# A decoder layer whose routed expert results are added to their token rows by accumulating transfers, with half of the shared expert moved ahead of the routed tiles

## The chip, the cores and the metric

The kernel runs on one NeuronCore of a Trainium2 chip. The metric is the device time of one execution in microseconds (us), taken as the median of several runs. One further execution was recorded by the hardware profiler, and every duration below is from that one. The engines are named as in the profile: PE is the matmul engine (PEld its weight loads), DVE the vector engine, ACT the scalar engine, POOL the GpSimd engine, SP the engine that only issues transfers. An engine's name with a q behind it (SPq, ACTq) is its queue of transfers.

## What is computed

One decoder layer on 32 blocks of 128 tokens, 256 wide: causal attention with 16 heads, a retention-like second attention, and a mixture of experts, each added to its input and normalised. The change concerns only the last part:

```python
x = _layernorm(x + _L0_attn_ref(x, L0_attn_qkv_weights), axis=-1)
x = _layernorm(x + _L0_xattn_ref(x, ctx_1024, ctx_1024, ...), axis=-1)
x = _layernorm(x + _L0_ffn_ref(x, ...), axis=-1)
...
# _L0_ffn_ref: one shared expert, and the best 2 of 8 routed experts for each token
hs = jnp.einsum('bsd,ndf->nbsf', x, sw1) + sb1[:, None, None, :]
shared_out = jnp.einsum('nbsf,nfd->bsd', _swiglu(hs), sw2) + sb2.sum(0)
probs = jax.nn.softmax(x @ gate_w + gate_b, axis=-1)
topk_probs, topk_idx = jax.lax.top_k(probs, TOP_K)
cw = jnp.sum(jax.nn.one_hot(topk_idx, N_EXPERTS, dtype=x.dtype) * topk_probs[..., None], axis=2)
hr = jnp.einsum('bsd,edf->ebsf', x, rw1) + rb1[:, None, None, :]
out_e = jnp.einsum('ebsf,efd->ebsd', _swiglu(hr), rw2) + rb2[:, None, None, :]
routed_out = jnp.einsum('ebsd,bse->bsd', out_e, cw)
return shared_out + routed_out
```

All data are float32.

## The kernel before, in words

Every engine has its own program, written out by hand in the order in which it runs; semaphores join them. There are four stages.

**Attention**, about 0 to 401 us. Blocks of 128 tokens go through a pipeline of steps n = -2 to 40; step n works on several blocks at once, each at another depth. At the end of the pipeline a block has its second layernorm result x2, which goes as a packet (256 values, the row number of its first result, its two expert numbers) to two rows of the DRAM tensor `sent`, one for each of its experts, by indirect transfers of POOL (L640). The row with x2 and the bias sb2 goes to `x2_dram`, the transposed one to `x2T_dram`.

**The gap**, about 401 to 463 us. The last steps n = 33 to 40 empty the pipeline: they route the last blocks, and in steps 33 to 36 PE puts one piece (`shared_half`, L795) of the shared expert's first group between them. A group q is 4 blocks, 512 tokens; there are 8. Then DVE counts the rows of each expert (15 dependent operations, `planned`, L1447 to L1464), and PE computes the first layer of group 1.

**Routed tiles**, about 463 to 692 us. `sent` is worked through in 71 tiles of 128 rows, each of one expert. For tile i: a load of ACT's queue brings the packets (`xg`), PE transposes them (L976), ACT copies them out (L1184), PE multiplies by rw1 (`hidden`, L990), DVE adds the bias (L1486), ACT takes the Silu (L1179), POOL multiplies (`product`, L671), PE transposes (L983), ACT copies (L1189), PE multiplies by rw2 (`result`, L1001), DVE adds the bias (`yg`, L1505), and POOL writes the 128 result rows to their places in the DRAM tensor `back` by an indirect transfer (`send_back`, L674). The tiles overlap: in PE's queue turn_x(i+1), turn_h(i-1), result(i-2) and hidden(i+1) follow each other. Two `back` transfers may be under way at once.

**The tail**, 692 us to the end. For each group, the results (`got`, 1 MB) and the rows x2 are loaded, DVE multiplies and sums them with the token's weights (`weighted`, L1548), adds the shared expert's output (`add_shared`, L1566), takes the moments, POOL the root (L697), ACT normalises and SP stores. PE computes the shared expert's first layer of groups 2 to 7 (`shared`, L795) and second layer of groups 0 to 7 (`output`, L1039) here, with the two engines handing each other PSUM banks.

## Time and profile before

| | us |
|---|---|
| median of 3 runs | 769.59 (768.74 to 775.72) |
| the profiled execution, its own time | 775.48 |
| its span from first to last instruction | 773.6 |
| PE busy | 705.6 (91%) |
| DVE busy | 499.1 (65%) |
| ACT busy | 410.3 (53%) |
| POOL busy | 319.1 (41%) |

The profiled execution took 5.9 us more than the median of the runs. A sum made against it is carried to the median by taking off that difference. Matmuls are pipelined, so a busy PE is not PE at its peak.

### The profile page before, as it was taken

Reading aid. Unit: us, or ns where it says so; the run is one execution under the profiler, and the core shown is the slowest. Engines: PE = TensorE matmul, PEld = TensorE weight load, DVE = VectorE, ACT = ScalarE, POOL = GpSimd, SP = SyncE. Lnnn points to the kernel's source line nnn. Section 1 sums busy time; section 2 is a strip of 40 time slices with the busy share of each in tenths; the row PEclk is TensorE's granted clock in tenths of the full one; section 3 lists DMA queues with packets and bytes.
Section 4 is the critical chain, followed back from the end, with each engine's and each line's share of the span. In section 5 each row is a group of like instructions: output and inputs, shape, how many; then the busy total and the mean of one; then the engine's idle time right before and its main releaser. Section 6 shows DMA issues by size and latency. Waiting matters only on the chain.

```text
span 773.6 us, 19404 instructions
## 1 busy us (share of the span) xinstructions
PE 705.6 (91%) x5464; PEld 533.1 (69%) x5465; DVE 499.1 (65%) x1568; ACT 410.3 (53%) x1167; POOL 319.1 (41%) x451
## 2 busy tenths in 40 slices
PE   6978899999999999999987639999999999999993
PEld 6857788888888888888875315666666666665453
DVE  3555678888988888898866432444444444438985
ACT  0268688888888888888851102333333333312233
POOL 1001233335554554455455542555555555541111
PEclk9999999999999999999999677999999999999998
DMA  8644462213332332333271432422222222229962
GB/s 290 253 145 157 138 223 74 83 57 106 102 97 82 103 109 77 100 101 108 85 228 62 151 124 88 152 83 88 83 87 89 82 89 84 86 61 320 302 215 81
DMA packets 77032, 97.54 MB, mean 126 GB/s; under 512 B 12320, under 2 KB 63264, under 8 KB 75936
## 3 DMA queue, kind: packets, MB, share of 16 engines
q1 hardware_dynamic: 59920, 68.21, 28.0%
q0 software_dynamic: 6816, 19.00, 6.8%
q10 hardware_dynamic: 10224, 9.42, 4.4%
q8 instruction: 39, 0.64, 0.3%
q14 instruction: 33, 0.27, 0.1%
HBM read 60.02 MB, written 36.56 MB: 125 GB/s over the span
## 4 chain that ended last, share of the span: by engine, by line
PE 67%; issue 14%; DVE 5%; SPq 5%; DMA 4%; POOL 2%; ACT 1%; POOLq 0%; ACTq 0%; DVEq 0%
PE ps L990 16%; PE ps L1001 8%; PE ps L777 5%; PE ps L765 4%; PE ps L855 4%; PE ps L742 4%; PE ps L787 4%; PE ps L879 3%; PE ps L745 3%; PE ps L858 3%; PE ps L976 2%; PE ps L983 2%; DMA attn_only<-in_ctx 2%; DVE products L1263 2%; PE ps L865 2%
## 5 line engine op out<-in xcount | busy, mean ns | idle before, releaser
L1079 ACT ACTIVATE prob<-ps,nmax 128x128 f32<-128x128 f32 x512 | 146.8, 378 | 30.2 <-DVE nmax L1253 30.2
L990 PE MATMUL ps<-first_use,xgT 128*128 x284 | 137.3, 607 | 1.3 <-ACT xgT L1184 1.2
L1486 DVE TENSOR_TENSOR hid<-ps,attn_only 128x512 f32<-128x512 f32 x71 | 49.1, 692 | 93.8 <-PE ps L990 93.8
L1184 ACT COPY xgT<-ps 128x256 f32<-128x256 f32 x71 | 26.5, 373 | 133.9 <-PE ps L976 131.7
L1253 DVE TENSOR_REDUCE nmax<-ps 128x4 f32<-128x512 f32 x128 | 82.2, 685 | 22.7 <-PE ps L765 21.0
L671 POOL TENSOR_TENSOR gate_h<-hid,sil 128x256 f32<-128x256 f32 x71 | 50.9, 717 | 100.3 <-DVE result_row L1499 82.7
L1086 ACT COPY pT<-ps 128x512 f32<-128x512 f32 x128 | 76.7, 599 | 19.2 <-PE ps L777 14.5
L621 POOL TENSOR_TENSOR rot<-products 128x128 f32<-128x128 f32 x128 | 61.2, 499 | 60.9 <-DVE products L1263 57.8
L777 PE MATMUL ps<-tf,prob 128*128 128x128 f32 x512 | 78.6, 276 | 5.8 <-ACT pT L1086 5.7
L990 PEld LDWEIGHTS ps<-first_use,xgT 128*128 128x128 f32 x284 | 54.7, 194 | 41.1 <-issue 37.5
L640 POOL DMA_INDIRECT sent<-packets,pos x64 | 63.6, 994 | 37.1 <-PE ps L765 22.8
L674 POOL DMA_INDIRECT back<-yg,result_row x71 | 71.8, 1011 | 13.8 <-issue 12.3
L1001 PE MATMUL ps<-first_use,ghT 128*128 x284 | 74.0, 383 | 0.5 <-ACT ghT L1189 0.5
L777 PEld LDWEIGHTS ps<-tf,prob 128*128 128x128 f32 x512 | 59.3, 141 | 11.7 <-issue 5.4
L795 PE MATMUL ps<-prob,sw_sb 128*128 128x512 f32 x128 | 62.5, 639 | 3.9 <-DMA prob<-x2T_dram 2.7
L976 PEld LDWEIGHTS ps<-tf,xg 128*128 128x128 f32 x142 | 19.1, 144 | 54.9 <-issue 54.2
L1505 DVE TENSOR_TENSOR yg<-ps,attn_only 128x256 f32<-128x256 f32 x71 | 30.2, 425 | 39.3 <-PE ps L1001 36.7
L1001 PEld LDWEIGHTS ps<-first_use,ghT 128*128 128x128 f32 x284 | 48.3, 190 | 4.9 <-issue 0.9
L1263 DVE TENSOR_TENSOR products<-ps,tf 128x256 f32<-128x256 f32 x128 | 46.3, 404 | 6.0 <-PE ps L879 2.0
L795 PEld LDWEIGHTS ps<-prob,sw_sb 128*128 128x128 f32 x128 | 25.5, 203 | 33.4 <-issue 29.2
L653 POOL TENSOR_TENSOR rstd<-mv,neg_half 128x1 f32<-128x1 f32 x32 | 17.7, 552 | 67.5 <-DVE mv L1271 67.5
L1359 DVE CAST ps<-tb 128x512 f32<-128x512 bf16 x62 | 42.0, 682 | 2.1 <-ACT prob L1079 2.1
(135 smaller groups left out, 1390.2 us busy)
## 6 DMA issues: line engine op xcount, KB each, us to landing
xg<-sent ACTq DMA_DIRECT2D x68, 129.5 KB
first_use<-back SPq DMA_DIRECT2D x8, 1024.0 KB, 8.2
k_dram<-first_use SPq DMA_DIRECT2D x4, 1024.0 KB, 4.3
attn_only<-in_x_turned SPq DMA_DIRECT2D x32, 128.0 KB, 2.7
attn_only<-k_dram SPq DMA_DIRECT2D x256, 16.0 KB
attn_only<-in_x SPq DMA_DIRECT2D x32, 128.0 KB, 2.6
attn_only<-in_ctx SPq DMA_DIRECT2D x32, 128.0 KB, 2.6
first_use<-in_L_ffn_rw SPq DMA_DIRECT2D x8, 512.0 KB, 5.0
```

The lines of the kernel that those rows point to most:

```text
L621: eng.tensor_tensor(rot[:, t % 2, m + e, :], ra[:, t % 2, m + e, :], rb[:, t % 2, m + 1 - e, :], ALU.add).then_inc(done, 1)
L640: eng.indirect_dma_start(sent, bass.IndirectOffsetOnAxis(ap=pos[:, t, j:j + 1], axis=0), packets[:, t % SLOTS, :], None).then_inc(sent_in[ ...
L671: eng.tensor_tensor(gate_h[:, r, :], hid[:, r, FFN:2 * FFN], sil[:, r, :], ALU.mult).then_inc(gh_set, 1)
L674: eng.indirect_dma_start(back, bass.IndirectOffsetOnAxis(ap=result_row[:, slot:slot + 1], axis=0), yg[:, slot % 2, :], None).then_inc(yg_o ...
L777: mm = eng.transpose(PROBT[:, n * P:(n + 1) * P], prob[:, t % 2, 4 * u + n, :], ident)
L795: mm = eng.matmul(ps[:, bank0 + 2 * f + half, :].rearrange("p (b t) -> p b t", b=QB), sw1_sb[:, c, cols:cols + P], x2T4[:, r, :, c, :], st ...
L990: mm = eng.matmul(ps[:, r, :], xgT[:, r, c, :], rw1_sb[:, bass.ds(e * (DC * 2 * FFN) + c * 2 * FFN, 2 * FFN)], start=(c == 0), stop=(c == ...
L1001: mm = eng.matmul(ps[:, 4 + r, 0:D], ghT[:, r, c, :], rw2_sb[:, bass.ds(e * (FFN // P * D) + c * D, D)], start=(c == 0), stop=(c == FFN // ...
L1079: ins = eng.activation(prob[:, t % 2, 4 * u + n, :], SCORE[u][:, n * P:(n + 1) * P], ACT.Exp, bias=nmax[:, t % 2, 4 * u + n:4 * u + n + 1])
L1086: eng.copy(pT[:, u, :, :].rearrange("p n t -> p (n t)"), PROBT).then_inc(pT_set, 1)
L1253: eng.tensor_reduce(nmax[:, t % 2, 4 * u:4 * u + 4], SCORE[u].rearrange("p (h j) -> p h j", j=P), AX_X, ALU.max, negate=True).then_inc(max ...
L1263: eng.tensor_tensor(into[:, t % 2, m:m + 2, :], source, table[:, m:m + 2, :], ALU.mult).then_inc(done, 1)
```

## The change

**Results.** The tensor `back` goes. A new DRAM tensor `total` has one row for each token (and 128 rows for padding); it holds x2 plus sb2 first, and for groups 0 to 3 (`EARLY` is 4) the shared expert's output too. DVE and POOL work out each row's weight from two more values in the packet, ACT multiplies the tile's result by it (`weighted`, into `yw`), and POOL's indirect transfer adds the 128 rows to `total` (`add_rows`, with an accumulate operation). Since two tiles can hold the same token, a tile's transfer is issued only when the one before has landed: `wait_rows(i)` waits for `row_added` to reach 16*i. The issue comes three tiles behind `product`, one tile later than before.

**Shared expert.** PE computes both layers of groups 0 to 3 before the tiles: between the last steps of the pipeline (`shared_between`, steps 33 to 39) and beside DVE's counting. DVE adds them to the rows `kept` in SBUF, and SP stores these. Groups 4 to 7 come behind the tiles.

**Tail.** When all 71 additions have landed SP loads `total` in 8 pieces of 512 KB. Nothing is left to be weighted; DVE adds the shared output of groups 4 to 7 alone, and takes the moments of all 8.

```diff
-PACKET = D + 3
+PACKET = D + 5
...
+        total = nc.dram_tensor("total", (ROWS + P, D), F32).ap()
...
-        back = nc.dram_tensor("back", (PADDING + TILES * P, D), F32).ap()
...
+            def store_kept(q):
+                eng.wait_ge(sy_added, 2 * q + 2)
+                eng.dma_start(total[q * QB * S:(q + 1) * QB * S, :].rearrange("(b p) d -> p b d", p=P),
+                              kept[:, q * QB:(q + 1) * QB, :]).then_inc(kept_stored, 16)
+            for q in range(EARLY - 2):
+                store_kept(q)
             eng.wait_ge(plan_step, PLAN_STEPS)
...
+            eng.wait_ge(row_added, 16 * TILES)
+            for q in range(NQ):
+                eng.dma_start(fin[:, q * QB:(q + 1) * QB, :],
+                              total[q * QB * S:(q + 1) * QB * S, :].rearrange("(b p) d -> p b d", p=P)).then_inc(fin_in[q], 16)
...
-            def product(i, r, more=True):
+            def product(i, r):
                 eng.wait_ge(sil_set, i + 1)
                 after(eng, gh_turned, i - 1)
-                if more:
-                    eng.wait_ge(yg_set, i - 1)
-                    eng.wait_ge(packet_row, i - 1)
                 eng.tensor_tensor(gate_h[:, r, :], hid[:, r, FFN:2 * FFN], sil[:, r, :], ALU.mult).then_inc(gh_set, 1)
-            def send_back(slot):
-                eng.indirect_dma_start(back, bass.IndirectOffsetOnAxis(ap=result_row[:, slot:slot + 1], axis=0),
-                                       yg[:, slot % 2, :], None).then_inc(yg_out[slot % 2], 16)
-            for i in range(2):
-                product(i, i, more=False)
-            for i in range(2, 4):
+            def tile_weight(i, slot):
+                eng.wait_ge(part_set, i + 1)
+                eng.tensor_tensor(weight[:, slot:slot + 1], weight_part[:, slot:slot + 1], xg[:, slot, D + 3:D + 4],
+                                  ALU.add).then_inc(weight_set, 1)
+            def wait_rows(i):
+                eng.wait_ge(yw_set, i + 1)
+                eng.wait_ge(packet_row, i + 1)
+                after(eng, row_added, 16 * i)
+            def add_rows(slot):
+                eng.indirect_dma_start(total, bass.IndirectOffsetOnAxis(ap=result_row[:, slot:slot + 1], axis=0),
+                                       yw[:, slot % 2, :], None, compute_op=ALU.add).then_inc(row_added, 16)
+            for i in range(3):
                 product(i, i % 2)
-                send_back(i - 2)
+                tile_weight(i, i)
+            for r in range(2):
+                eng.wait_ge(x2_stored[r], 16 * (B - EARLY * QB) // 2)
+            eng.wait_ge(idle_sent, 32)
+            eng.wait_ge(kept_stored, 16 * EARLY)
+            product(3, 1)
+            wait_rows(0)
+            tile_weight(3, 3)
+            add_rows(0)
             with eng.Fori(1, TILES // 4) as k:
                 for n in range(4):
                     product(4 * k + n, n % 2)
-                    send_back((n - 2) % 4)
+                    wait_rows(4 * k + n - 3)
+                    tile_weight(4 * k + n, n)
+                    add_rows((n + 1) % 4)
             for i in range(TILES // 4 * 4, TILES):
                 product(i, i % 2)
-                send_back((i - 2) % 4)
-            for i in range(TILES - 2, TILES):
-                eng.wait_ge(yg_set, i + 1)
-                eng.wait_ge(packet_row, i + 1)
-                send_back(i % 4)
-            def root(q, r):
+                wait_rows(i - 3)
+                tile_weight(i, i % 4)
+                add_rows((i - 3) % 4)
+            for i in range(TILES - 3, TILES):
+                wait_rows(i)
+                add_rows(i % 4)
...
+            def shared_hidden(q, f, bank):
+                if q > 0:
+                    eng.wait_ge(sgh_set, 2 * (q - 1) + f + 1)
+                for half in range(2):
+                    shared_half(q, f, half, bank)
+            def shared_output(q, bank):
+                eng.wait_ge(sgh_set, 2 * q + 2)
+                for i in range(2):
+                    if 0 < q < EARLY:
+                        eng.wait_ge(sy_added, 2 * (q - 1) + i + 1)
+                    for b in (2 * i, 2 * i + 1):
+                        for c in range(FFN // P):
+                            mm = eng.matmul(ps[:, bank + i, b % 2 * D:(b % 2 + 1) * D], sgh[:, q % 2, c, b * P:(b + 1) * P],
+                                            sw2_sb[:, c, :], start=(c == 0), stop=(c == FFN // P - 1))
+                    mm.then_inc(sy_made, 1)
+            def shared_between(n):
                 if n == B + 1:
-                    eng.wait_ge(x2T4_in[0], 16)
                     eng.wait_ge(ffn_in, 16 * (2 + 2 * NE))
                     eng.wait_ge(expd, 4 * B)
-                    shared_half(0, 0, 0)
+                    shared_hidden(0, 0, 0)
                 if n == B + 2:
-                    shared_half(0, 0, 1)
+                    shared_hidden(0, 1, 2)
                 if n == B + 3:
-                    shared_half(0, 1, 0)
+                    shared_hidden(1, 0, 0)
                 if n == B + 4:
-                    shared_half(0, 1, 1)
+                    eng.wait_ge(pT_set, 4 * B)
+                    eng.wait_ge(att_set, B)
+                    shared_output(0, 4)
+                if n == B + 5:
+                    shared_hidden(1, 1, 2)
+                if n == B + 6:
+                    shared_hidden(2, 0, 0)
+                if n == B + 7:
+                    shared_output(1, 4)
...
+            shared_hidden(2, 1, 2)
+            shared_hidden(3, 0, 0)
+            shared_output(2, 4)
+            shared_hidden(3, 1, 2)
+            shared_output(3, 4)
             eng.wait_ge(base_set, len(GROUPS) + 1)
-            shared(1, 0, 1, 4)
-            eng.wait_ge(sgh_set, FFN // P)
+            eng.wait_ge(res2_set, B)
+            eng.wait_ge(sgh_set, 2 * EARLY)
+            eng.wait_ge(sy_added, 2 * EARLY)
...
             result(TILES - 2, TILES % 2, two_before)
-            output(0, 0, 2)
+            eng.wait_ge(sgh_set, 2 * EARLY)
+            shared_half(EARLY, 0, 0, 6)
             turn_h(TILES - 1, (TILES - 1) % 2)
-            output(0, 0, 3)
             result(TILES - 1, (TILES - 1) % 2, before)
-            eng.wait_ge(yg_set, TILES - 1)
-            output(0, 0, 1)
+            shared_half(EARLY, 0, 1, 6)
+            eng.wait_ge(hid_set, TILES)
+            shared_hidden(EARLY, 1, 0)
+            shared_hidden(EARLY + 1, 0, 6)
+            eng.wait_ge(xgT_set, TILES)
+            eng.wait_ge(ghT_set, TILES)
+            shared_output(EARLY, 2)
+            shared_hidden(EARLY + 1, 1, 0)
+            shared_hidden(EARLY + 2, 0, 6)
             eng.wait_ge(yg_set, TILES)
-            output(0, 0, 0)
-            for r in range(2):
-                shared(2 + r, 1, r)
-                outputs(1 + r, 1 - r)
-            with eng.Fori(2, NQ // 2) as k:
-                for r in range(2):
-                    shared(2 * k + r, k, r)
-                    outputs(2 * k + r - 1, 1 - r)
-            outputs(NQ - 1, 1)
+            shared_output(EARLY + 1, 4)
+            shared_hidden(EARLY + 2, 1, 0)
+            shared_hidden(EARLY + 3, 0, 6)
+            eng.wait_ge(sy_added, 2 * EARLY + 2)
+            shared_output(EARLY + 2, 2)
+            shared_hidden(EARLY + 3, 1, 0)
+            eng.wait_ge(sy_added, 2 * EARLY + 4)
+            shared_output(EARLY + 3, 4)
...
+            def weighted(i, r, slot):
+                eng.wait_ge(yg_set, i + 1)
+                eng.wait_ge(weight_set, i + 1)
+                after(eng, row_added, 16 * (i - 1))
+                eng.activation(yw[:, r, :], yg[:, r, :], ACT.Copy, scale=weight[:, slot:slot + 1]).then_inc(yw_set, 1)
...
+            def add_shared(q, bank):
+                if q < EARLY:
+                    eng.wait_ge(x2b_set, (q + 1) * QB)
+                else:
+                    eng.wait_ge(fin_in[q], 16)
+                for i in range(2):
+                    rows = (kept if q < EARLY else fin)[:, q * QB + 2 * i:q * QB + 2 * i + 2, :].rearrange("p b d -> p (b d)")
+                    eng.wait_ge(sy_made, 2 * q + i + 1)
...
-            def pad_rows(i, slot, loads):
+            def weight_parts(i, slot, loads):
                 eng.wait_ge(xg_in[slot], loads * 16)
-                eng.scalar_tensor_tensor(out=pad_shift[:, slot:slot + 1], in0=xg[:, slot, D:D + 1], scalar=float(PADDING),
-                                         in1=tile_rows[:, bass.ds(i, 1)], op0=ALU.is_ge, op1=ALU.mult).then_inc(pad_shifted, 1)
-                eng.scalar_tensor_tensor(out=packet_at[:, slot:slot + 1], in0=tile_e[:, bass.ds(i, 1)],
-                                         scalar=xg[:, slot, D + 2:PACKET], in1=xg[:, slot, D:D + 1],
-                                         op0=ALU.is_equal, op1=ALU.add).then_inc(pad_shifted, 1)
-            def packet_rows(i, slot):
-                eng.wait_ge(pad_shifted, 2 * i + 2)
-                eng.tensor_tensor(result_row[:, slot:slot + 1], pad_shift[:, slot:slot + 1], packet_at[:, slot:slot + 1],
-                                  ALU.add).then_inc(packet_row, 1)
-            def out_y(i, r, sent_before, e):
+                eng.scalar_tensor_tensor(out=weight_part[:, slot:slot + 1], in0=tile_e[:, bass.ds(i, 1)],
+                                         scalar=xg[:, slot, D + 2:D + 3], in1=xg[:, slot, D + 4:D + 5],
+                                         op0=ALU.is_equal, op1=ALU.mult).then_inc(part_set, 1)
+            def rows_of(i, slot):
+                after(eng, row_added, 16 * (i - 3))
+                eng.tensor_copy(result_row[:, slot:slot + 1], xg[:, slot, D:D + 1]).then_inc(packet_row, 1)
+            def out_y(i, r, e):
                 eng.wait_ge(yg_made, i + 1)
-                after(eng, yg_out[r], sent_before * 16)
+                after(eng, yw_set, i - 1)
...
+            def moments(q):
+                if q < EARLY:
+                    eng.wait_ge(fin_in[q], 16)
+                for b in range(QB):
+                    if q >= EARLY:
+                        eng.wait_ge(sy_added, 2 * q + b // 2 + 1)
+                    eng.bn_stats(bn3[:, q, b, :], fin[:, q * QB + b, :]).then_inc(bn3_set, 1)
+                eng.wait_ge(bn3_set, (q + 1) * QB)
+                for b in range(QB):
+                    eng.bn_aggr(mv3[:, q, b, :], bn3[:, q, b, :]).then_inc(mv3_set, 1)
+                eng.wait_ge(mv3_set, (q + 1) * QB + q)
+                eng.tensor_scalar(var3[:, q, :], mv3[:, q, :, 1], EPS, None, ALU.add).then_inc(mv3_set, 1)
...
+            shared_gate(4, 0, 6)
+            shared_gate(4, 1, 0)
+            shared_gate(5, 0, 6)
+            moments(0)
+            shared_gate(5, 1, 0)
+            moments(1)
+            shifts(0)
+            add_shared(4, 2)
```

The order on **POOL, in the loop over the tiles**, two tiles of the four in a turn before and one now. `gate_h` is the product, `back` and `total` the transfers; in the new kernel `tile_parts` holds `gate_h`, `oT` holds `yw`. Before:

```order
L671 TENSOR_TENSOR gate_h<-hid,sil 128x256 [waits packet_row,yg_set,gh_turned]
L674 DMA back<-yg,result_row 17280x256
L665 REGISTER_ALU
L671 TENSOR_TENSOR gate_h<-hid,sil 128x256 [waits yg_set,packet_row,gh_turned,sil_set]
L674 DMA back<-yg,result_row 17280x256
```

Now:

```order
L636 REGISTER_ALU
L638 TENSOR_TENSOR tile_parts<-tile_parts 128x256 [waits gh_turned,sil_set]
L411 REGISTER_ALU [waits packet_row,yw_set]
L642 TENSOR_TENSOR weight<-weight_part,xg 128x1 [waits part_set,row_added]
L654 DMA total<-oT,result_row 4224x256
```

The wait for the transfer before (`row_added`) and a small addition now stand between the product and the transfer.

The order on **PE, in steps 35 to 39, around the last two routing counts** (L938 before, L944 now). Before:

```order
L925 MATMUL ps<-gate_w_sb,x2T 128x8
L938 MATMUL ps<-picks,tb 128x16 [waits gc_set,base_set,picks_set]
L942 MATMUL ps<-picks,tb 128x8
L946 MATMUL ps<-picks,tb 128x8 x2
L938 MATMUL ps<-picks,tb 128x16 [waits gc_set,base_set,picks_set]
L942 MATMUL ps<-picks,tb 128x8
L946 MATMUL ps<-picks,tb 128x8 x2
L795 MATMUL ps<-prob,sw_sb 128x512 [waits x2T4_in1,base_set]
```

Now (L784 is the first layer, L804 the second):

```order
L931 MATMUL ps<-gate_w_sb,x2T 128x8
L784 MATMUL ps<-prob,sw_sb 128x512 [waits sgh_set]
L784 MATMUL ps<-prob,sw_sb 128x512 x3
L944 MATMUL ps<-picks,tb 128x16 [waits gc_set,base_set,picks_set]
L948 MATMUL ps<-picks,tb 128x8
L952 MATMUL ps<-picks,tb 128x8 x2
L784 MATMUL ps<-prob,sw_sb 128x512 [waits x2T4_in2,sgh_set]
L784 MATMUL ps<-prob,sw_sb 128x512 x3
L804 MATMUL ps<-sw_sb,tile_parts 128x256 [waits sy_added,sgh_set]
L804 MATMUL ps<-sw_sb,tile_parts 128x256 x3
L804 MATMUL ps<-sw_sb,tile_parts 128x256 [waits sy_added]
L804 MATMUL ps<-sw_sb,tile_parts 128x256 x3
```

Behind the gate's matmul of the last block two first-layer pieces and a second layer now stand ahead of the last count.

The order on **DVE, in the counting** (`planned`): before, its 15 operations stood in a row and the gates (L1472) behind them. Now a gate (L1389) stands inside:

```order
L1509 CAST counts<-counts_i 128x8 [waits plan_step]
L1389 SCALAR_TENSOR_TENSOR tile_parts<-ps,sb_sb,pT 128x512 [waits sy_made,ssil_set,plan_step]
L1511 TENSOR_TENSOR upto<-counts,tf 128x64
L1513 TENSOR_REDUCE counts<-upto 128x8 [waits plan_step]
L1514 TENSOR_SCALAR counts<-counts 128x8 [waits plan_step]
L1515 TENSOR_TENSOR passed<-counts,tf 128x568 [waits plan_step]
L1517 TENSOR_REDUCE tile_f<-passed 128x71 [waits plan_step]
L1389 SCALAR_TENSOR_TENSOR tile_parts<-ps,sb_sb,pT 128x512 [waits sy_made,ssil_set,plan_step]
L1519 TENSOR_SCALAR tile_e<-tile_f 128x71
L1520 CAST tile_expert<-tile_e 1x71 [waits plan_step]
```

Two gates now stand between the counting operations, each of which waits for ACT and so for PE.

## Rows read from the trace of the kernel before

**Rows 1.** The page's busy line and its row of PE's granted clock (40 slices).

```profile
PE 705.6 (91%) x5464; PEld 533.1 (69%) x5465; DVE 499.1 (65%) x1568; ACT 410.3 (53%) x1167; POOL 319.1 (41%) x451
...
PEclk9999999999999999999999677999999999999998
```

**Rows 2.** Busy time by stretch: PE, PEld, DVE, ACT, POOL, clock, DMA share, GB/s.

```profile
401.00:463.00 62.00, 36.30 (x170) 22.25 (x170) 28.62 (x124) 8.05 (x17) 32.77 (x42) 0.81 0.37 121
463.00:503.00 40.00, 38.39 (x127) 21.80 (x128) 14.56 (x53) 11.58 (x33) 15.28 (x18) 0.87 0.40 119
503.00:684.00 181.00, 181.00 (x709) 111.84 (x708) 81.38 (x295) 61.91 (x177) 101.97 (x118) 1.00 0.28 85
684.00:692.30 8.30, 7.76 (x35) 5.59 (x34) 2.38 (x9) 1.05 (x3) 4.98 (x6) 1.00 0.14 49
692.30:762.00 69.70, 66.51 (x210) 39.24 (x208) 58.99 (x182) 20.01 (x36) 7.48 (x8) 1.00 0.72 243
762.00:773.60 11.60, 0.00 (x0) 0.00 (x0) 2.53 (x12) 4.15 (x8) 1.03 (x2) 0.72 0.26 90
```

**Rows 3.** Timeline of one tile: start, us, engine, line.

```profile
522.34 1.01 POOL L674 DMA_INDIRECT back<-yg,result_row  x1 [0.16 <-issue]
...
523.48 1.88 PE L990 MATMUL ps<-first_use,xgT 128*128 x4
...
523.81 0.42 DVE L1505 TENSOR_TENSOR yg<-ps,attn_only 128x256 f32<-128x256 f32 x1 [0.42 <-PE ps L1001]
...
524.48 0.72 POOL L671 TENSOR_TENSOR gate_h<-hid,sil 128x256 f32<-128x256 f32 x1 [1.12 <-DVE result_row L1499]
...
525.36 1.01 POOL L674 DMA_INDIRECT back<-yg,result_row  x1 [0.16 <-issue]
...
526.50 1.88 PE L990 MATMUL ps<-first_use,xgT 128*128 x4
```

**Rows 4.** Timeline: the last `back` transfer, and SP's first instruction that waited for it.

```profile
691.74 0.96 POOL L674 DMA_INDIRECT back<-yg,result_row  x1 [1.53 <-DVE yg L1505]
...
694.16 0.91 SPq L540 DMA_DIRECT2D first_use<-back  x2
```

**Rows 5.** POOL's groups by shape: busy us, mean ns of one, idle before.

```profile
L621 POOL TENSOR_TENSOR rot<-products 128x128 f32<-128x128 f32 x128 | 61.2, 499 | 60.9 <-DVE products L1263 57.8 <-issue 2.7
L671 POOL TENSOR_TENSOR gate_h<-hid,sil 128x256 f32<-128x256 f32 x71 | 50.9, 717 | 100.3 <-DVE result_row L1499 82.7 <-ACT sil L1179 17.5
...
L653 POOL TENSOR_TENSOR rstd<-mv,neg_half 128x1 f32<-128x1 f32 x32 | 17.7, 552 | 67.5 <-DVE mv L1271 67.5
```

**Rows 6.** Timeline: the first loads of `xg` from DRAM, and PE, which waited for the first.

```profile
460.87 2.60 SPq L554 DMA_DIRECT2D xg<-sent  x3
...
463.04 0.66 PE L976 MATMUL ps<-tf,xg 128*128 128x128 f32 x2 [11.81 <-DMA xg<-sent]
```

**Rows 7.** Timeline of the gap.

```profile
433.19 3.32 PE L795 MATMUL ps<-prob,sw_sb 128*128 128x512 f32 x4
...
437.74 1.28 ACT L1156 ACT_TABLE_LOAD   x1
...
440.88 0.19 PE L938 MATMUL ps<-picks,tb 128*128 128x16 bf16 x1 [2.06 <-issue]
...
454.40 0.22 DVE L1464 TENSOR_TENSOR tile_row<-tile_f,tf 1x71 int32<-1x71 f32 x1 [0.67 <-DVE tile_f L1463]
...
458.66 0.69 ACT L1156 ACTIVATE pT<-ps,sb_sb 128x512 f32<-128x512 f32 x1 [10.15 <-remote]
```

**Rows 8.** Timeline of the tail on PE: first layer, second layer, and the last one.

```profile
737.73 7.03 PE L795 MATMUL ps<-prob,sw_sb 128*128 128x512 f32 x16
...
744.60 3.62 PE L1039 MATMUL ps<-sw_sb,products 128*128 128x256 f32 x16
...
754.92 7.07 PE L1039 MATMUL ps<-sw_sb,products 128*128 128x256 f32 x32
```

**Rows 9.** DVE's groups from 440 us on: the weighting of half of the results.

```profile
L1548 DVE SCALAR_TENSOR_TENSOR first_use<-first_use,cw 128x256 f32<-128x256 f32 x32 | 13.3, 479 | 2.0 <-DMA first_use<-back 2.0
```

426 lines of the change are left out of this document (182 added, 244 removed).

## The prediction

> **What bounds the kernel now.** Read the busy line first: PE is busy for 705.6 of 773.6 us, and its granted clock is full but for three of the forty slices, around 430 to 480 us [rows 1]. Then go by stages [rows 2]. In the attention and in the tiles PE does not rest: from 503 to 684 us it is busy for all of the 181 us, at clock 1.00. A tile takes 12 matmul passes (four of L990, four of L1001, two each of L976 and L983), so 709 passes are 59.1 tiles, and a tile takes 181 / 59.1 = 3.06 us. The start of one tile's L990 to the next tells the same, 526.50 - 523.48 = 3.02 [rows 3]. POOL is busy for 102 of these 181 us; nobody waits for its transfers. Two places are not at PE's limit. In the gap, 401 to 463 us, PE is busy for 36.3 of 62 us at a mean clock of 0.81. In the tail it is busy for 66.5 of 69.7 us, but DVE is busy for 59.0 of them, and 11.6 us follow in which PE has ended and the last group is normalised and stored [rows 2]. So the tail costs 762.0 + 11.6 - 692.3, 81.3 us, and PE's share of it is what the change moves.
>
> **The tail gets shorter: -27 us.** Now PE computes first layers of six groups and second layers of eight there. The first layer of a group takes 7.03 us and the second 3.62 [rows 8]. Afterwards four groups are left: 4 x (7.03 + 3.62) = 42.6 us. They start in the slots at 687.5 that now hold group 0's second layer. Added to them are the last two tiles' results and transposes with the wait for ACT's copy, about 2.4 us, and one wait for the last Silu and gate, about 1.8. PE then ends at 687.5 + 46.8 = 734.3 where it ends at 762.0 now: 27.7 us less, and I take 27. The 11.6 us behind it stay: moments, root, normalising and storing of one group are the same. DVE loses the weighting, 64 operations of 479 ns, 30.7 us (half of them are in [rows 9]), so it cannot bound the tail. What is new there is the load of `total`, 4.2 MB in eight pieces, behind the last addition. Its cover is PE's queue: groups 4 and 5 need no row of it for their first layers, some 20 us. If the cover fails, because the last additions land late, DVE stands at `moments(0)` with the gates of group 5 queued behind it, and PE waits for these; I price that at 0 to 12 us and take 0.
>
> **The gap gets longer: +9 us.** Ahead of the last routing count PE now has two more first-layer pieces, 3.5 us each by half of 7.03, and one second layer, 3.6: 10.6 us [rows 8]. Their cover is PE's idle time there, 2.06 us ahead of that count [rows 7] and about as much ahead of the one before; 6.5 us remain, and DVE's counting waits for them. The Silu pieces now alternate with the Exp of the routing. A change of table costs 1.28 us [rows 7]; there is one now and there will be five. Of the four new ones I put 2 us on the path. Two gates stand inside the counting, 0.75 us each, and the first waits for PE's piece and ACT: 3 us. Against it, the first-layer passes at 433.19 took 3.32 us for four [rows 7], where four passes of the same width take 1.88 in a tile [rows 3]: PE had been idle and was at the lower clock level (1.2 GHz). With more work it may stay at 2.4 GHz, and I give 3 us back. The sum is 6.5 + 2 + 3 - 3 = 8.5, taken as 9. Behind the counting stand DVE's gate, a second layer and an addition, some 6.5 us; the way from its last operation at 454.40 to the first tile at 463.04 [rows 7, 6] takes 8.6 us anyway and hides them. The bounds are +3 and +16: ACT's Silu at 458.66 stood for 10.15 us on something the profile calls remote [rows 7], and if that hits a gate inside the counting, 7 us come on top.
>
> **The tiles: +43 us.** PE's work for a tile is unchanged. ACT has one more operation of 0.4 us, DVE one fewer; neither is near its limit (62 and 81 of 181 us, rows 2). The two new values in a packet and the small operations that fill them in the attention cost nothing that can be seen: PE bounds it. What is new is a ring. An addition may be issued only when the one before has landed, and in POOL's queue the next product stands behind that wait. One turn of the ring is: the transfer from its issue to its landing, POOL's small addition L642, and 0.16 us ahead of the issue [rows 3]. The last `back` transfer was issued at 691.74, and SP went on at 694.16: 2.42 us [rows 4]. A POOL operation takes 717 ns on 256 columns and 499 on 128 [rows 5], which leaves 0.28 for one column; a root of one column takes 0.55. So the ring would turn in 2.42 + 0.16 + 0.28 to 0.55 = 2.86 to 3.13 us if an adding transfer were as quick as a writing one. I take 3.0. That is PE's 3.06 already, with nothing to spare.
>
> An adding transfer must also read its 128 rows. The trace has none. From below this costs nothing, if the read lies beside the other parts of the transfer. It can't be a gain, since the same bytes are written. From above it is a whole trip to DRAM: 128 packets were loaded in 463.04 - 460.87 = 2.17 us [rows 6]. I take a third, 0.7 us: issue, first fetch and the receipt are shared with the write, and only the rows' own way is added. The ring then turns in 3.7 us, and the stage grows by (3.7 - 3.06) x 68 = 43.5 us (three of the 71 additions start before the ring is full). The product of the next tile, 0.72 us [rows 3], fits into the transfer's flight, so it adds nothing. DVE's `rows_of` and ACT's `weighted` wait for the same landings; from a landing through bias, Silu and product to the next issue there are two turns, so they do not set the pace.
>
> The start of the tiles, 463 to 503 us, ran at 0.87 of the clock and lost some 7 us with its filling [rows 2]. A PE that comes busy out of the gap loses less: -2 us.
>
> The Trainium skill says of a transfer on POOL's path that it costs about 2.0 us plus its bytes at 436 GB/s (DMA: Bandwidth & Descriptors, "Anatomy of one DMA"); for 128 KB an estimate by that page is 2.3 us, and [rows 4] show 2.42 with the waiting engine's own delay. The same page ("SDMA does more than copy") says that the units which add are inline with the data stream. By that rule the addition would be free but for the read, and the time that of the first rival below. Its rules for kernel authors say too that an accumulate reads its destination and writes it later, so that the next must wait for the earlier one's semaphore; no row here shows such a transfer.
>
> **The sum.** 43.5 - 27 + 9 - 2 = +23.5. The profiled execution took 775.5 us, so 799.0; it was 5.9 above the median, which makes 793.
>
> **Rivals.** *The additions hide* (chance 0.27): the read lies beside the write, the ring turns in at most PE's 3.06 us, and 9 - 27 - 2 = -20 remain: 750 us. For it speaks that the ring without the read is 2.86 at the least; against it that this leaves 0.2 us. *The ring is only just too slow* (0.13): 3.2 to 3.4 us a turn, +10 to +23 - 20, that is 760 to 773. At 3.35 us gain and loss are equal. *The additions are serial* (0.18): each row is read, added and written before the next, or POOL needs longer to write the descriptors. With the whole trip of 2.17 on top of 3.0 the ring turns in 5.2 us: +145 - 20, 895 us; I count everything above 4.3 us a turn, 834 us, to this case. This one is decided at the same place as my forecast and is its far end. *The tail does not shrink* (0.02 with everything else): if the load of `total` blocks the gates, 12 of the 27 us are lost; that shifts any of the cases and does not decide the sign alone.
>
> **How the numbers follow.** My forecast, a ring of 3.4 to 4.3 us (773 to 834 us), has 0.40, and is the likeliest; 793 is its time. A difference under 1% (762 to 777 us) can't be told from none. Faster by more than that: the additions hide, and a little of the next case, 0.28. Within it: 0.14. Slower: 0.58. Both signs have much, so the forecast's own range is 773 to 834, and the one that should hold the time 8 times in 10 reaches from 746 (additions hidden, gap at +5) to 858 (ring at 4.65 us).
>
> **What would show it.** In the profile after: the distance from one L654 to the next in the tiles. At 3.06 with PE busy throughout the first rival is right; at 3.7, with PE some 17% idle and POOL waiting for `row_added`, I am. PE's first tile should start at 472 instead of 463, with the counting's end near 463. From the last tile's result to the end there should be 57 us instead of 84, and a few more if the last additions land late. I would be wrong in the size if the read costs under 0.35 or over 1.3 us, and wrong in the mechanism if PE slows in the tiles while POOL waits for something else than `row_added`, or if the clock falls there because PE rests each turn.

## The result, and the profile after

The changed kernel takes 840.80 us (median of 4 runs, 836.48 to 843.58), the kernel before 769.77 beside it (4 runs): a ratio of 1.0915, with a 95% interval of 1.0871 to 1.0960. It is 71 us slower, where 23.5 were forecast. The profiled execution took 842.12 us, with a span of 839.9; the spans of the two profiles differ by only 66.3 us, since the one before was of an execution 5.7 us above its median. Of all the runs below one fell into a slower state, a run of `half_count` with 1444.54 us, and it is left out there.

The page of the changed kernel, from its busy line to the costliest groups (out<-in xcount | busy, mean ns of one | idle time before):

```profile
PE 725.7 (86%) x5464; PEld 527.5 (63%) x5465; DVE 470.1 (56%) x1427; ACT 450.1 (54%) x1242; POOL 372.9 (44%) x523
...
PEclk9988999999999999999899899999999999999996
...
q0 software_dynamic: 13680, 19.20, 13.1%
...
L654 POOL DMA_INDIRECT total<-oT,result_row x71 | 112.1, 1579 | 21.9 <-issue 9.7
...
L1205 ACT ACTIVATE oT<-yg,weight 128x256 f32<-128x256 f32 x71 | 36.1, 508 | 127.3 <-DMA total<-oT,result_row 126.6
...
L1547 DVE CAST result_row<-xg 128x1 uint32<-128x1 f32 x71 | 10.9, 153 | 125.6 <-DMA total<-oT,result_row 125.6
```

PE's share fell from 91 to 86% [rows 1], and of the dip of its granted clock to 0.6 and 0.7 around the gap two slices at 0.8 are left. Two engines stood for about 126 us each on one thing, the landing of an addition. Two more numbers belong to it: POOL needs 1.58 us to issue an adding transfer, where it needed 1.01 for a writing one [rows 3], and the software queue has 13680 packets. The page of the kernel before has this for the queue:

```profile
q0 software_dynamic: 6816, 19.00, 6.8%
```

The bytes are nearly the same, the packets twice as many, and the DMA engines' time on them twice as much (6.8% of 773.6 us, 13.1% of 839.9).

Busy time by stretch, in the columns of [rows 2]. The first line is of the kernel before, the others are of the changed one:

```profile
430.00:463.00 33.00, 14.26 (x42) 6.56 (x42) 14.20 (x62) 4.51 (x7) 18.79 (x20) 0.75 0.39 139
...
430.00:463.00 33.00, 31.18 (x120) 18.75 (x119) 20.62 (x91) 8.41 (x12) 21.13 (x23) 1.00 0.60 193
...
503.00:766.00 263.00, 207.03 (x742) 109.89 (x743) 83.41 (x248) 95.95 (x248) 152.89 (x185) 1.00 0.39 62
766.00:792.60 26.60, 21.19 (x61) 10.92 (x60) 5.76 (x14) 6.34 (x14) 11.50 (x11) 0.94 0.26 30
792.60:829.70 37.10, 31.70 (x93) 19.04 (x91) 21.46 (x81) 15.35 (x29) 7.09 (x7) 0.91 0.56 184
```

In the end of the gap PE is busy for 31 of 33 us at clock 1.00, where it was busy for 14 at 0.75. In the tiles it is busy for 207 of 263 us, at full clock: it waits, and its clock does not fall for it. One turn in the timeline:

```profile
599.38 1.58 POOL L654 DMA_INDIRECT total<-oT,result_row  x1 [0.15 <-issue]
599.83 0.35 ACTq L1184 DMA_DIRECT2D xg<-sent  x1
...
600.78 1.98 PE L1001 MATMUL ps<-first_use,xgT 128*128 x4 [0.95 <-ACT xgT L1194]
...
601.22 0.71 POOL L638 TENSOR_TENSOR tile_parts<-tile_parts 128x256 f32<-128x256 f32 x1 [0.26 <-ACT tile_parts L1189]
...
603.21 0.15 DVE L1547 CAST result_row<-xg 128x1 uint32<-128x1 f32 x1 [2.07 <-DMA total<-oT,result_row]
603.21 0.51 ACT L1205 ACTIVATE oT<-yg,weight 128x256 f32<-128x256 f32 x1 [1.82 <-DMA total<-oT,result_row]
603.26 0.19 POOL L642 TENSOR_TENSOR weight<-weight_part,xg 128x1 f32<-128x1 f32 x1 [1.32 <-DMA total<-oT,result_row]
603.60 1.57 POOL L654 DMA_INDIRECT total<-oT,result_row  x1 [0.15 <-issue]
...
604.99 0.30 PEld L1001 LDWEIGHTS ps<-first_use,xgT 128*128 128x128 f32 x2 [1.33 <-issue]
```

The issue at 599.38, three engines released at 603.21 to 603.26, the next issue at 603.60: 4.22 us. Over the stage, one line of all L654 says it for 61 turns, (761.9 - 502.0) / 61 = 4.26 us:

```profile
L654 POOL DMA_INDIRECT total<-oT,result_row x62: 1572/1581/1592, 502.0 to 761.9; - x62
...
DMA to landing us min/median/max: 3.6/3.8/4.0
```

The gap's end and the tail, from the timelines of PE, DVE, POOL and SP:

```profile
450.61 0.17 PE L944 MATMUL ps<-picks,tb 128*128 128x16 bf16 x1
...
463.22 0.22 DVE L1524 TENSOR_TENSOR tile_row<-tile_f,tf 1x71 int32<-1x71 f32 x1
...
465.57 2.60 SPq L555 DMA_DIRECT2D xg<-sent  x3
...
471.96 0.41 PE L987 MATMUL ps<-tf,xg 128*128 128x128 f32 x2 [1.09 <-DVE kept L1400]
...
778.30 1.13 PE L1010 MATMUL ps<-first_use,ghT 128*128 x4 [0.56 <-ACT ghT L1199]
...
789.73 1.55 POOL L654 DMA_INDIRECT total<-oT,result_row  x1 [3.02 <-DMA total<-oT,result_row]
...
793.28 7.43 SPq L565 DMA_DIRECT2D first_use<-total  x8
...
823.28 6.46 PE L804 MATMUL ps<-sw_sb,tile_parts 128*128 128x256 f32 x16 [4.99 <-DVE tile_parts L1389]
```

The last result of the tiles in the kernel before:

```profile
689.66 1.03 PE L1001 MATMUL ps<-first_use,ghT 128*128 x4
```

The spans differ by 839.9 - 773.6 = 66.3 us. By stage that is: the first tile starts at 471.96 for 463.04 [rows 6], +8.9; the tiles, (4.26 - 3.06) x 68 = +81.6; from the last tile's result to the end 61.6 us for 83.9, -22.3; and -2 is what remains. The forecast had -2 for a start of the tiles that loses less, but this -2 is a remainder and was not measured there.

### The profile page after: what moved, and what is told of

Same layout as the page of the kernel before. It is cut to its first block, busy times and chain, and to the rows that moved or that the text cites. A ratio compares the mean times of both kernels' runs of the same rounds, so it can differ in the third digit from the quotient of the medians.

```text
span 839.9 us, 19432 instructions
## 1 busy us (share of the span) xinstructions
PE 725.7 (86%) x5464; PEld 527.5 (63%) x5465; DVE 470.1 (56%) x1427; ACT 450.1 (54%) x1242; POOL 372.9 (44%) x523
## 3 DMA queue, kind: packets, MB, share of 16 engines
q0 software_dynamic: 13680, 19.20, 13.1%
## 4 chain that ended last, share of the span: by engine, by line
PE 50%; DMA 18%; issue 13%; DVE 6%; POOL 6%; ACT 3%; ACTq 2%; SPq 1%; POOLq 0%; DVEq 0%
DMA total<-oT,result_row 14%; PE ps L764 5%; POOL total L654 5%; PE ps L1001 4%; PE ps L861 4%; PE ps L752 4%; PE ps L774 4%; PE ps L729 4%; PE ps L885 3%; PE ps L864 3%; PE ps L732 3%; PE ps L804 2%; PE ps L695 2%; PE ps L784 2%; PE ps L871 2%
## 5 line engine op out<-in xcount | busy, mean ns | idle before, releaser
L1001 PE MATMUL ps<-first_use,xgT 128*128 x284 | 142.9, 626 | 53.3 <-ACT xgT L1194 53.3
L654 POOL DMA_INDIRECT total<-oT,result_row x71 | 112.1, 1579 | 21.9 <-issue 9.7
L1001 PEld LDWEIGHTS ps<-first_use,xgT 128*128 128x128 f32 x284 | 49.0, 191 | 114.6 <-issue 114.5
L1205 ACT ACTIVATE oT<-yg,weight 128x256 f32<-128x256 f32 x71 | 36.1, 508 | 127.3 <-DMA total<-oT,result_row 126.6
L1536 DVE TENSOR_TENSOR tile_parts<-ps,attn_only 128x512 f32<-128x512 f32 x71 | 49.1, 692 | 72.5 <-issue 59.7
L1547 DVE CAST result_row<-xg 128x1 uint32<-128x1 f32 x71 | 10.9, 153 | 125.6 <-DMA total<-oT,result_row 125.6
L638 POOL TENSOR_TENSOR tile_parts<-tile_parts 128x256 f32<-128x256 f32 x71 | 52.1, 733 | 47.3 <-ACT tile_parts L1189 47.3
L764 PEld LDWEIGHTS ps<-tf,prob 128*128 128x128 f32 x512 | 59.4, 142 | 12.7 <-issue 5.0
L784 PE MATMUL ps<-prob,sw_sb 128*128 128x512 f32 x128 | 58.8, 607 | 1.8 <-DVE tile_parts L1389 1.8
L642 POOL TENSOR_TENSOR weight<-weight_part,xg 128x1 f32<-128x1 f32 x71 | 13.4, 189 | 84.9 <-DMA total<-oT,result_row 79.8
L987 PEld LDWEIGHTS ps<-tf,xg 128*128 128x128 f32 x142 | 16.7, 143 | 53.9 <-issue 43.3
```

What stands on the lines that cost most here:

```text
L638: eng.tensor_tensor(gate_h[:, r, :], hid[:, r, FFN:2 * FFN], sil[:, r, :], ALU.mult).then_inc(gh_set, 1)
L654: eng.indirect_dma_start(total, bass.IndirectOffsetOnAxis(ap=result_row[:, slot:slot + 1], axis=0), yw[:, slot % 2, :], None, compute_op=A ...
L764: mm = eng.transpose(PROBT[:, n * P:(n + 1) * P], prob[:, t % 2, 4 * u + n, :], ident)
L784: mm = eng.matmul(ps[:, bank + half, :].rearrange("p (b t) -> p b t", b=QB), sw1_sb[:, c, cols:cols + P], x2T4[:, q % EARLY, :, c, :], sta ...
L1001: mm = eng.matmul(ps[:, r, :], xgT[:, r, c, :], rw1_sb[:, bass.ds(e * (DC * 2 * FFN) + c * 2 * FFN, 2 * FFN)], start=(c == 0), stop=(c == ...
L1536: eng.tensor_tensor(hid[:, r, :], ps[:, r, :], rb_h[:, bass.ds(e * (2 * FFN), 2 * FFN)], ALU.add).then_inc(hid_set, 1)
```

## The experiments

The runs were made in three groups, each beside runs of the kernel before on its own chip (medians 775.62, 771.52 and 774.74 us), so ratios are compared. The ratios are those on record; they are not the quotients of the medians and differ from these by up to 0.4%.

### Writing in place of adding

```
-  yw[:, slot % 2, :], None, compute_op=ALU.add).then_inc(row_added, 16)
+  yw[:, slot % 2, :], None).then_inc(row_added, 16)
```

> The changed kernel with one word out: the transfer of a tile's rows to `total` writes and does not add. All waits stay, the ring too. It leaves out the summing of the two results of a token. Theory A (what an adding transfer costs more is its longer issue on POOL, 1.58 for 1.01 us, and its read, together 1.4 us a turn): the issue goes back to 1.0 us, the way from issue to landing to 2.4, the ring would turn in 2.42 + 0.19 + 0.23 = 2.84 us, PE's 3.06 bounds again, and the time is 841 - 1.2 x 68 = 759 us, within 4. Theory B (the waiting itself is dear: the three engines that wait for one landing and start again behind it): the turn stays above 3.4 us and the time above 785.

Measured: 790.15 us, ratio 1.0156 (1.0105 to 1.0207). The issue is back at 1.01 us, but a turn takes (718.5 - 500.2) / 62 = 3.52 us, not PE's 3.06. By its numbers that is theory B: a ring costs something even where it writes. What it costs is seen in the timeline:

```profile
603.38 1.01 POOL L654 DMA_INDIRECT total<-oT,result_row  x1
...
603.83 0.35 ACTq L1184 DMA_DIRECT2D xg<-sent  x1
...
606.53 0.51 ACT L1205 ACTIVATE oT<-yg,weight 128x256 f32<-128x256 f32 x1 [1.14 <-DMA total<-oT,result_row]
```

From issue to landing 3.15 us, where the last transfer of the kernel before took 2.42 [rows 4]. The load of the next tile is issued 0.45 us behind each transfer, since ACT's load stands in its queue behind the weighting, and the weighting waits for the landing before. The trace's packet records tell more. For each transfer between 520 and 680 us I took, from the start of its issue, the start of its first packet and the end of its last; the table has the medians of these, in us. The ns are the mean of a packet, the packets of 4 bytes left out; the last column is the first packet of the `xg` load beside it:

```
kernel             issue  first  last  packets of a transfer   ns of one  xg load
before              1.01   1.59  2.10   32 of 4096 bytes          180        -
plain_write         1.01   1.99  2.73   32 of 4096 bytes          159       1.42
plain_load_ahead    1.01   1.58  2.09   32 of 4096 bytes          178     earlier
changed kernel      1.58   2.16  3.49  128 of 1024 bytes          143       1.41
half_rows           1.58   2.16  3.04  128 of 512 bytes            91       1.41
half_count          1.44   2.06  2.96   64 of 1024 bytes          150       1.41
```

In `plain_write` the load's packets run from 1.42 to 2.41, ahead of the transfer's and beside them, which so begin 0.4 us late and last longer. No engine is slow to go on, as theory B had it: from the last packet to ACT's start are 0.36 to 0.38 us in every kernel in which ACT waits for it. In the changed kernel the load's packets end at 2.19, when the addition's first (2.16) has only just begun.

### The load ahead of the weighting

```
+  if not last:
+      load(i + 3, (n + 3) % 4)
   if not (first and n < 2):
       weighted(i - 2, n % 2, (n - 2) % 4)
-  if not last:
-      load(i + 3, (n + 3) % 4)
```

> The same move of the load in the kernel whose transfer writes and does not add (the sum of a token's two results is left out). There a turn took 3.49 us, and a landing 3.1 us of it where the last transfer of the kernel before took 2.4. Theory D: the landing falls to 2.5, the ring would turn in 2.9 us, PE's 3.06 bounds, the time falls by 0.43 x 68 = 29 us to a ratio of 0.98. Theory E: the turn stays at 3.4 to 3.5 us and the ratio at 1.015.

> The changed kernel with ACT's load of tile i+3 ahead of the weighting of tile i-2 in its queue, not behind it. In the changed kernel the weighting waits for a landing, so the next load is issued 0.45 us behind every issue of an addition, and its packets start 1.41 us behind that issue, ahead of the addition's own (2.16 to 3.49 us behind it). Theory D (the load collides with the transfer in each turn, because the ring has put them in step): the load moves to the end of the flight, the addition's packets start at 1.8 us, a turn falls from 4.26 to 3.9 us and the time by 24 us against the changed kernel, a ratio to the kernel before of 1.06. Theory E (the start of the packets is a matter of the issue alone): the turn stays at 4.2 and the ratio at 1.09.

Measured, writing: 755.30 us, ratio 0.9786 (0.9737 to 0.9835), a turn of (678.0 - 500.1) / 58 = 3.07 us. Theory D holds there: moving one load gave back 0.45 us a turn. Its rows (landing is from issue to the waiting engine):

```profile
L654 POOL DMA_INDIRECT total<-oT,result_row x59: 1007/1008/1018, 500.1 to 678.0; - x59
...
DMA to landing us min/median/max: 2.5/2.5/2.5
```

Measured, adding: 836.66 us, ratio 1.0845 (1.0798 to 1.0892), a turn of (746.1 - 500.2) / 58 = 4.24 us. There theory D is wrong: the addition's packets still start 2.15 us behind the issue. The collision is a fact of the writing ring, not of the adding one. Written or added, the first packet comes 0.57 us behind the end of the issue (1.01 + 0.57 = 1.58, 1.58 + 0.57 = 2.15), so it is the longer issue that delays the addition.

### Half the bytes, half the rows

```
half_rows:   total.rearrange("r (h d) -> (r h) d", h=2), ... yw[:, slot % 2, 0:P]
half_count:  ... ap=result_row[0:64, slot:slot + 1] ... yw[0:64, slot % 2, :]
```

> The changed kernel with additions of half the width: 128 rows of 512 bytes instead of 1024, of the first half of each row, to a view of `total` in rows of that width, so that the sums are left out. Theory A1 (issue and landing go by the number of rows): the issue stays at 1.58 us and a turn at 4.1 to 4.26, the time at 830 to 841. Theory A2 (the 0.84 us beyond the issue are bytes on their way, read and written): half of it goes, a turn is 3.8 us and the time 841 - 0.42 x 68 = 812.

Measured: 816.62 us, ratio 1.0489 (1.0427 to 1.0552):

```profile
L654 POOL DMA_INDIRECT total<-oT,result_row x63: 1572/1582/1593, 502.2 to 739.3; - x63
```

The issue is unchanged, a turn is 237.1 / 62 = 3.82 us. That is theory A2. The packets account for it: eight of them on each of 16 DMA engines, 143 - 91 = 52 ns less each, 0.42 us. With half the bytes a packet took 91 ns and not half of 143, so a part of its time does not go by the bytes.

> The changed kernel with additions of 64 rows of 1024 bytes in place of 128 (the other 64 results of a tile are left out of the sums). In the trace a whole addition's issue takes 1.58 us, its first packet starts 0.57 us behind the issue's end, the packets last 1.33 us, and the waiting engines go on 0.37 us later. Theory G (issue and packets both go by the number of rows): the issue falls to 0.8 to 1.0 us and the packets to 0.7, the landing to 2.5 to 2.7, a turn would be 2.9 to 3.1 and PE bounds: 841 - 1.15 x 68 = 763 us, a ratio of 0.98 to 1.0. Theory H (the issue costs the same for any number of rows, only the packets halve): 1.58 + 0.57 + 0.67 + 0.37 = 3.2, a turn 3.6, 796 us and a ratio of 1.03.

Measured: 810.15 us (3 runs), ratio 1.0443 (1.0387 to 1.0499):

```profile
L654 POOL DMA_INDIRECT total<-oT,result_row x64: 1427/1439/1466, 499.7 to 736.1; - x64
```

A turn is 236.4 / 63 = 3.75 us. Half the rows take only 0.14 us off the issue, so between 64 and 128 rows nearly all of it stays; the packets last 0.90 us for 1.33. It lies near theory H, above its 3.6 and its 796 us, since H had the packets at 0.67. Theory G is out.

### The product in the ring

```
+  wait_rows(4 * k + n - 3)
   product(4 * k + n, n % 2)
-  wait_rows(4 * k + n - 3)
   tile_weight(4 * k + n, n)
```

> The changed kernel with the product of a tile on POOL moved from ahead of the wait for the last landing to behind it, so that it lies in the ring. Theory A (the ring is the chain landing, POOL's operations, issue, landing, and nothing else sets the pace): a turn grows by the product's 0.72 us less the 0.08 of its start, 4.26 to 4.9, and the time by 0.64 x 68 = 44, to 884 us. Theory C (the pace is set in the DMA queue, which takes the transfers at its own rate, or by a chain over PE and ACT): the turn grows by less than 0.3 us, and the time stays under 862.

Measured: 903.13 us, ratio 1.1639 (1.1563 to 1.1714), a turn of (818.5 - 498.5) / 63 = 5.08 us: +0.82 for a product of 0.72. Theory A holds, with 0.18 more a turn than the 0.64 that it gave, and 903 us for its 884. What is put in the ring is paid in full, and here with 0.1 us beyond the product that stays open.

### Two additions in flight

To keep two additions on their way without two of them meeting in a row, even and odd tiles got a total and a semaphore each. The second is zeroed in the attention and added in the tail, so the results are the whole computation's.

```
-  indirect_dma_start(total, ...).then_inc(row_added, 16)
+  indirect_dma_start([total, total2][slot % 2], ...).then_inc(row_added[slot % 2], 16)
```

> The changed kernel with two tensors in place of `total`: even tiles add to one and odd tiles to the other, each with its own semaphore, so an addition waits for the last but one. The second is zeroed during the attention, and POOL adds it to the first in the tail, 1024 columns a group. Theory A (the wait for the landing sets the pace, and transfers can lie beside each other): a ring of 4.3 to 5.0 us holds two tiles, POOL's own work for a tile is 0.72 + 0.19 + 1.58 + 0.5 = 3.0 us, PE's 3.06 bounds again; 841 - 1.2 x 68 = 759, plus 0 to 6 for the tail's adding: 756 to 765. Theory C (the queue takes adding transfers one after the other): an addition lands 3.8 us behind the last one however it is issued, the tiles stay at 3.8 us and more, and the time is above 805.

Measured: 811.67 us, ratio 1.0452 (1.0360 to 1.0544), (732.5 - 499.4) / 63 = 3.70 us a tile. The tile is a little under theory C's 3.8 us and the time is in C's range (above 805), far from the 756 to 765 of theory A. But the waits show another cause than C's. Those of its tiles (us in all, times, longest):

```profile
ACT oT L1228 <- DMA total<-oT,result_row: 66.7, 54, 2.3
...
POOL tile_parts L651 <- ACT tile_parts L1212: 63.7, 58, 2.2
```

POOL no longer waits for landings. ACT does: there are two buffers of weighted rows, so the weighting of tile i waits for the addition of tile i-2, with the next tile's Silu behind it.

> The kernel with two totals, and four buffers of weighted rows in place of two, so that ACT's weighting no longer waits for the last but one landing. With two buffers a tile took 3.71 us, ACT waited 67 us for landings and POOL 64 us for ACT's Silu behind it. Theory F (the wait of the weighting, with Silu and load queued behind it on ACT, is a second ring): a tile falls to 3.1 or 3.2 us and the time by 38 us, a ratio to the kernel before of 0.99 to 1.01. Theory C (the DMA queue or POOL can't take an adding transfer in under 3.6 us): the tile stays at 3.6 and the ratio at 1.04.

Measured: 801.34 us, ratio 1.0409 (1.0332 to 1.0485), and (719.3 - 499.0) / 60 = 3.67 us a tile. Theory F failed by its numbers, which are theory C's. But the wait had left ACT and come up on DVE, in `rows_of`, whose four slots make it wait for the addition of tile i-4, issued only one tile earlier:

```profile
DVE result_row L1577 <- DMA total<-res,result_row: 38.3, 28, 2.9
...
DVE result_row L1577 <- DMA total<-oT,result_row: 32.5, 18, 2.7
```

> Two totals, four buffers of weighted rows, the sum of the weight on DVE instead of POOL, the product on POOL behind the wait for the last but one landing (which is then over), and the second total added on DVE in the tail instead of POOL. Theory F: POOL needs 0.72 + 1.58 + 0.3 = 2.6 us a tile, PE's 3.06 bounds; against the kernel before the tail gives 27 less some 10 for the second total, the gap costs 9, so -8 to -15 us, a ratio of 0.98 to 0.99. Theory C: a tile takes 3.6 us and the ratio is 1.03.

Measured: 798.41 us, ratio 1.0376 (1.0307 to 1.0445), (713.0 - 500.0) / 60 = 3.55 us a tile. Again these are theory C's numbers (3.6 us, 1.03) and not F's. The wait is the same one:

```profile
POOL tile_parts L652 <- ACT tile_parts L1198: 63.1, 37, 2.5
ACT tile_parts L1198 <- DVE tile_parts L1553: 55.0, 44, 3.0
...
DVE result_row L1569 <- DMA total<-res,result_row: 27.1, 29, 2.0
...
DVE result_row L1569 <- DMA total<-oT,result_row: 20.9, 16, 1.6
```

Read from below: DVE stands in `rows_of` (48.0 us in all), the bias of the next tile is queued behind it, ACT's Silu waits for the bias, POOL's product for the Silu. The next run takes this wait away, by the edit below, and has the tail's loads in another order:

```
-  rows_of(i, n, 2 * k + n // 2 - 1)
+  rows_of(i - 1, (n - 1) % 4, 2 * k + (n - 1) // 2 - 1)
```

> The last kernel with two edits. DVE takes tile i-1's result rows in step i and not tile i's, so that the wait for a free slot of result rows is for an addition issued two tiles ago and not one (there DVE waited 48 us in 46 waits for landings, with the next tile's bias queued behind them). And the tail loads and adds the second total in the order in which the groups are finished (0, 1, 4, 2, 5, 3, 6, 7; DVE had waited 4.35 us for group 4's rows). Theory F (each wait for a landing that is younger than 3.9 us holds the tile back, on whatever engine it stands): a tile falls from 3.58 to 3.06 to 3.15 us, the time by 33 + 4, a ratio to the kernel before of 0.98 to 0.995. Theory C (the queue or POOL can't take additions at that rate): a tile stays at 3.5 us, the ratio at 1.03.

Measured: 774.11 us (12 runs) beside 774.74 (17 runs), ratio 0.9988 (0.9959 to 1.0016). A tile takes (697.1 - 500.1) / 62 = 3.18 us, and PE is busy for nearly the whole stage:

```profile
503.00:684.00 181.00, 178.62 (x687) 105.35 (x686) 84.72 (x286) 87.01 (x229) 130.78 (x115) 1.00 0.48 83
```

So theory C, that the queue or POOL can't take the additions at that rate, is out. Theory F's mechanism is right, though both numbers lie just outside its ranges (3.06 to 3.15 us, a ratio of 0.98 to 0.995), and a tile is still 0.12 us above the 3.06 of the kernel before. The kernel only comes level with that one: its last issue is 18.0 us later (709.7 for 691.7 [rows 4]), and the way from there to the end is 22.5 us shorter (59.4 for 81.9). The changed kernel needs only 50.2 for it (789.7 to 839.9). The 9.2 us between the two go with the second total, which must be loaded (4.2 MB more) and added (1.22 us of DVE for each of eight groups); no run separates the parts. No version that computes the whole result was faster than the kernel before.

## Why the prediction was wrong in size

**What bounds now.** Right: a ring from issue to landing in the tiles, with PE at full clock and idle a fifth of the time. `product_behind` shows that a term put in the ring is paid in full, and `rows_later` shows that without it the tiles come to 3.18 us, near PE's 3.06.

**The ring's frame.** Forecast 2.42 + 0.16 + 0.42 = 3.0 us for a transfer that writes. The 2.42 were right ([rows 4]; 2.5 in `plain_load_ahead`). The small operation L642 takes 0.19 us and not 0.28 to 0.55, and 0.22 are between it and its neighbours: 2.83 in all, 0.17 too much.

**The failing step: "I take a third, 0.7 us: issue, first fetch and the receipt are shared with the write, and only the rows' own way is added."** An addition lands 3.85 us behind its issue, 1.4 more than a write, twice the 0.7. What failed is that the issue is shared. POOL needs 1.58 us for 1.01, and the first packet follows 0.57 behind its end in either kernel. That is 0.57 us which the sum had at nothing. The rows' own way, for which the 0.7 stood, came near: the packets last 1.33 us for 0.51, which is 0.82. Together 1.39, and 2.83 + 1.39 = 4.22, against a measured 4.26. With 4.26 in place of 3.7 the term is 81.6 us for 43.5: 38 of the 43 us between the forecast of the span's growth (23.5) and its 66.3.

The sign that the prediction named for a wrong size, a cost of over 1.3 us, is there. The time of 840.8 lies above the forecast's range (773 to 834), in what was given to the rival "The additions are serial"; the turn of 4.26 us is still under that rival's 4.3. The wider range, up to 858 us, held it. The longer issue was in the prediction only as that rival's half sentence ("or POOL needs longer to write the descriptors"), with no price of its own. `plain_write` shows that it goes with the adding, `half_count` that it is nearly the same for 64 rows.

Why do the packets last longer? Written, four rows travel in a packet; added, each row is one: 32 packets of 180 ns became 128 of 143, so a DMA engine is busy for 8 x 143 = 1.15 us and not 2 x 180 = 0.36. The cutting alone need not do it. In the trace of the changed kernel SP writes x2 to the same `total` without adding, 128 rows of 1024 bytes at a time:

```profile
418.01 0.32 SPq L515 DMA_DIRECT2D total<-x2b  x1
...
430.61 0.32 SPq L515 DMA_DIRECT2D total<-x2b  x1
```

By the packet records each of these two also goes in 128 packets of 1024 bytes, but of 47 ns each, and they last 0.52 us from the first to the last, as long as the 32 packets of a `back` transfer. That speaks for the adding as what makes the packets long, not their number. In an addition the first 16 packets take 310 ns each in the mean, and the last 96 take 108. It is not proof: SP's queue is another one and its rows lie side by side, and there is no run in which POOL's queue writes single scattered rows without adding. Nor is it shown whether the time goes into the read of the old row or into the adding itself.

By the rule of the Trainium skill that the units which add are inline with the data stream (DMA: Bandwidth & Descriptors, "SDMA does more than copy"), the addition would be free but for its read. The trace doesn't bear out that price for rows scattered by an index: 0.57 us of the cost come before any packet moves. It doesn't speak against the rule itself.

**The gap, +9.** Right as a sum, and in part by luck: the first tile starts at 471.96, forecast at 472, and the counting ends at 463.44, forecast "near 463". The last count came 9.7 us later (450.61 for 440.88, [rows 7]), more than the 6.5. From it to the counting's end it then took 12.83 us for 13.74, so the two gates, which were to add 3 us there, lengthened nothing that shows. The granted clock came as hoped, 1.00 for 0.75 from 430 to 463 us. And what ended last was not the way by the plan and the load, as forecast: the load was issued at 465.57, and with the 2.17 us of such a load [rows 6] I estimate that way to end near 467.7. It was the last addition of the shared expert (L1400, ahead of L987), which the forecast had held to be hidden.

**The tail, -27.** It measured -22.3. The last tile's result starts at 778.30 and the end is 61.6 us later, forecast 57. Mechanism and cover were named and the price taken at the wrong end, "0 to 12 us and take 0". The last three additions go one behind the other, 4.5 us each, so SP loads `total` only at 793.28. DVE and ACT then run late, PE waits 4.99 us for group 7's gate, and its last second layer takes 6.46 us where such a one took 3.62 [rows 8]: 7.8 us of loss there, part of which the forecast's own waits had covered. The granted clock from 820 to 830 us, behind that wait, is 0.66, where it was 1.00 from 810 to 820.

**The two together.** Forecast 9 - 27 - 2 = -20 without the ring. `plain_load_ahead`, where the ring holds at PE's pace, measured 755.30 - 771.52 = -16.2. It adds nothing up, so it is no kernel to use, but it shows that these terms hold to 4 us.

**"Two turns ... do not set the pace"** did no harm with one total. With two in flight it was wrong at once: two more waits for landings, in `weighted` and `rows_of`, each set the pace when the one ahead of it was gone.

## What to carry to other kernels

Price a new kind of transfer by its three stretches, issue, packets and receipt, and ask of each whether the row at hand had the same kind. The queue's line on the page of the profile gives packets, bytes and the engines' time, but more packets alone say little: here 128 plain ones took no longer than 32. A wait for the last landing turns a hidden latency into the period of the loop, so compare the whole turn with the bound of the busiest engine before the transfer's work. When one such wait is removed, look for the next older one on every in-order queue (buffers, index slots), and ask what transfers the wait has put in step.

## What the runs showed that I had not expected

An indirect transfer that writes sent 128 rows of 1024 bytes in 32 packets of 4096; with the addition each row is a packet, and such a packet takes 143 ns where a plain one of the same size, from SP's queue, takes 47. The issue of the addition is 1.58 us for 128 rows and 1.44 for 64, where the writing one takes 1.01 for 128. And in the writing ring, moving a 130 KB load from 0.45 us behind each transfer to ahead of it shortened the landing from 3.1 to 2.5 us and the kernel from a ratio of 1.016 to 0.979, with no work removed.
